# First layer norm and first projection of a two-layer transformer, written as one part

## The reference

```python
def _layernorm(x, axis=-1, eps=1e-05):
    m = jnp.mean(x, axis=axis, keepdims=True)
    v = jnp.var(x, axis=axis, keepdims=True)
    return (x - m) / jnp.sqrt(v + eps)
...
Q = (x @ W_q).reshape(b, s, N_HEADS, HEAD_DIM).transpose(0, 2, 1, 3)
K = (x @ W_k).reshape(b, s, N_KV_HEADS, HEAD_DIM).transpose(0, 2, 1, 3)
V = (x @ W_v).reshape(b, s, N_KV_HEADS, HEAD_DIM).transpose(0, 2, 1, 3)
Qr = _apply_rope(Q, positions)
...
Kr = _apply_rope(K_rep, positions)
```

## Time and profile before

| what | us |
|---|---|
| median of 3 runs | 2762.9 |
| lowest and highest run | 2759.66, 2764.67 |
| span of the profiled execution, first to last instruction | 2757.8 |
| median less span: what lies around the span | 5.1 |
| tensor engine busy | 2526.8 (92%) |
| vector engine busy | 1757.1 (64%) |
| from the start to the tensor engine's first instruction | 20.48 |
| from the start to the first product of the projection | 43.38 |
| from the start to the first tensor work of `heads0` | 141.15 |

### The profile page before, as it was taken

How to read it: one execution, slowest core, us unless ns; L and a number is a source line. 1 busy time by engine, 2 the same in 40 slices (tenths; PEclk the granted TensorE clock), 3 DMA queues, 4 the chain that set the end, 5 groups by cost and what they waited for, 6 DMA issues and landing times. The chain is left out here.

```text
span 2757.8 us, 35900 instructions
## 1 busy us (share of the span) xinstructions
PE 2526.8 (92%) x12212; PEld 1711.0 (62%) x12212; DVE 1757.1 (64%) x4109; ACT 1080.5 (39%) x2566; POOL 1022.2 (37%) x756
## 2 busy tenths in 40 slices
PE   5889989898869999999697999978999979999998
PEld 2334434343348888888575777756777656667886
DVE  4647757575435555555545999956999923335886
ACT  2125535353522333222223777725777721111111
POOL 2217758584911111110003676624445410001442
PEclk9969999999979999999899999999999999999999
DMA  7371211111020000000211101010000078883201
GB/s 252 131 180 24 54 24 40 26 35 31 2 106 16 16 15 15 15 16 1 85 50 54 62 29 28 23 40 24 9 9 16 1 259 295 295 294 93 58 24 62
DMA packets 167335, 193.64 MB, mean 70 GB/s; under 512 B 51982, under 2 KB 114446, under 8 KB 166784
## 3 DMA queue, kind: packets, MB, share of 16 engines
q1 hardware_dynamic: 155648, 178.90, 20.8%
q0 software_dynamic: 11520, 12.64, 1.4%
HBM read 161.95 MB, written 54.53 MB: 78 GB/s over the span
## 5 line engine op out<-in xcount | busy, mean ns | idle before, releaser
L621 DVE TENSOR_REDUCE mx<-bank 128x1 f32<-128x512 f32 x512 | 327.9, 679 | 121.7 <-PE bank L528 115.5
L468 POOL TENSOR_TENSOR probs<-probs 128x1024 f32<-128x1024 f32 x128 | 301.5, 2376 | 211.2 <-PE bank L551 174.0
L679 ACT ACTIVATE probs<-bank 128x1024 f32<-128x1024 f32 x256 | 250.1, 1022 | 271.8 <-PE bank L541 271.8
L1475 POOL TENSOR_SCALAR mix<-mix,sm 128x256 f32<-128x256 f32 (+1 forms) x256 | 232.5, 919 | 175.1 <-DVE sm L1372 174.9
L1415 ACT ACTIVATE ms<-ms,sm 128x256 f32<-128x256 f32 (+1 forms) x512 | 247.6, 486 | 93.9 <-DVE sm L1343 92.9
L528 PE MATMUL bank<-k_parts,q_parts 96*128 96x512 f32 x512 | 219.8, 476 | 7.3 <-DVE X L644 3.3
L528 PEld LDWEIGHTS bank<-k_parts,q_parts 96*128 96x128 f32 x512 | 94.0, 196 | 171.4 <-DVE mx L621 139.1
L855 POOL TENSOR_TENSOR up_lo<-up_raw,up_hi 128x1024 fp32r<-128x1024 f32 x16 | 46.2, 2907 | 401.0 <-ACT up_hi L845 401.0
L1343 DVE CUSTOM_DVE_ANT_0 ms<-bank,misc 128x256 f32<-128x256 f32 (+1 forms) x512 | 184.7, 399 | 2.3
L541 PE MATMUL bank<-q_parts,k_parts 97*128 97x512 f32 x512 | 148.4, 406 | 15.8 <-ACT probs L679 8.9
L925 DVE TENSOR_TENSOR hid<-bank,sg 128x512 f32<-128x512 f32 x64 | 44.2, 691 | 180.2 <-ACT sg L875 180.2
(11 more groups left out here) (221 smaller groups left out, 5863.4 us busy)
## 6 DMA issues: line engine op xcount, KB each, us to landing
ewg<-in_L_ffn_Wg_dram SPq DMA_DIRECT2D x32, 704.0 KB, 6.8
ewu<-in_L_ffn_Wu_dram SPq DMA_DIRECT2D x32, 704.0 KB, 8.0
ewd<-in_L_ffn_Wd_dram SPq DMA_DIRECT2D x32, 512.0 KB, 5.2
q_parts<-qk_dram SPq DMA_DIRECT2D x48, 256.0 KB, 4.4
up_raw<-in_L_ffn_W_dram SPq DMA_DIRECT2D x16, 512.0 KB, 4.1
ewd<-in_L_ffn_Wd_dram SPq DMA_DIRECT2D x32, 192.0 KB, 5.3
qk_dram<-qk_hi SPq DMA_DIRECT2D x4, 1280.0 KB, 5.1
qk_dram<-qk_lo SPq DMA_DIRECT2D x4, 1280.0 KB, 7.2
```

The source lines that it names most:

```text
L468: pool.tensor_tensor(probs[:, even, half, :], probs[:, even, half, :], probs[:, odd, half, :], ALU.add).then_inc(S["paired"], 1)
L621: dve.reduce_max(mx[:, U % 2, q, h:h + 1], bank[:, h, :], AX.X).then_inc(S["max"], 1)
L679: act.activation(probs[:, s % BUFS, 2 * x:2 * x + 2, :], bank[:, 2 + 2 * x:4 + 2 * x, :], ACT.Exp, scale=scale).then_inc(S["exps"], 1)
L1475: pool.tensor_scalar(mix[:, p % 2, h, 0:w], mix[:, p % 2, h, 0:w], sm[:, p % 3, 8 + h:9 + h], None, ALU.mult).then_inc(S["probs"], 1)
```

## The change: two blocks become one

The call of `layer_norm` ahead of `attention0` is gone; its work stands in `project0`. The second layer's `layer_norm` keeps its instructions, with the branches for the first one taken out. In the new block:

- The sync engine issues all loads at its start: X quarter 0, misc, the three weights, rope, X quarters 1 to 3, then the output weight and the second feed-forward weight.
- Moments, square root and reciprocal are taken per quarter of four tiles. For quarter 0 they run first, then its four tiles are normalised and transposed, and the products begin when the weights are there; rope is waited for apart, by the vector engine (`cos_in`).
- For quarter c+1 the vector engine takes the moments after turn 0 of quarter c, the reciprocal and two tiles after turn 1, one tile after turn 2 and one after turn 3. The tensor engine transposes one tile after each of the products 2 to 5, into two banks of their own (4 and 5).
- The values of quarter c are transposed after product 1 of quarter c+1, no longer at the end of quarter c.
- GpSimd issues the 16 clearing DMAs in quarter 2, three or four after each low half.

```diff
-            layer_norm(env, "0", first=True)
             attention0(env)
...
+            rows(0)
+            sp.dma_start(env["misc"][:, :], env["consts"]["misc"]).then_inc(consts_loaded, 16)
             for c0, c1, name in ((0, D, "W_q"), (D, D + P, "W_k"), (D + P, D + 2 * P, "W_v")):
                 sp.dma_start(w[:, :, c0:c1], ins["L0_attn_" + name].rearrange("(k p) n -> p k n", p=P)).then_inc(S["w"], 16)
-            sp.dma_start(rope[:, :, :], env["consts"]["rope0"].rearrange("p (a s) -> p a s", a=2)).then_inc(S["w"], 16)
+            sp.dma_start(rope[:, :, :], env["consts"]["rope0"].rearrange("p (a s) -> p a s", a=2)).then_inc(S["cos_in"], 16)
+            for c in range(1, NC):
+                rows(c)
...
         @block.tensor
         def _(pe):
-            wait(pe, S["w"], 64)
...
+            def turn_rows(n):
+                pe.wait_ge(xn_ready, n + 1)
+                if n >= 2:
+                    pe.wait_ge(xt_taken, n - 1)
+                for k in range(KD):
+                    mm = pe.transpose(bank[:, 4 + n % 2, k * P:(k + 1) * P], xn[:, n % 2, k * P:(k + 1) * P], ident)
+                mm.then_inc(xt_ready, 1)
...
+            pe.wait_ge(consts_loaded, 16)
+            for n in range(SUBS):
+                turn_rows(n)
+            wait(pe, S["w"], 48)
+            for c in range(NC):
+                pe.wait_ge(xt_taken, SUBS * (c + 1))
+                for f in range(NF):
+                    product(c, f)
+                    if f == 1 and c:
+                        turn_values(c - 1)
+                    if f >= 2 and c + 1 < NC:
+                        turn_rows(SUBS * (c + 1) + f - 2)
+            turn_values(NC - 1)
...
+            moments(0)
+            inverse(0)
+            for n in range(SUBS):
+                normal(n)
+            wait(dve, S["cos_in"], 16)
             for c in range(NC):
...
+                more = c + 1 < NC
+                for f in range(NR):
+                    turn(c, f)
+                    if more and f == 0:
+                        moments(c + 1)
+                    if more and f == 1:
+                        inverse(c + 1)
+                        normal(SUBS * (c + 1))
+                        normal(SUBS * (c + 1) + 1)
+                    if more and f in (2, 3):
+                        normal(SUBS * (c + 1) + f)
+                wait(dve, S["proj"], c * NF + NF)
+                wait(dve, S["v_rows"], c)
+                dve.tensor_copy(vT[:, :], bank[:, NR % 4, :]).then_inc(S["read"], 1)
...
                     wait(pool, S["hi"], c * NR + f + 1)
                     pool.tensor_tensor(lo[:, c % 2, f, :], rot[:, f % 2, :], hi[:, c % 2, f, :].bitcast(F32),
                                        ALU.subtract).then_inc(S["lo"], 1)
+                    if c == 2:
+                        for m in range(3 * f, min(3 * f + 4 if f == NR - 1 else 3 * f + 3, SLOTS // P)):
+                            pool.dma_start(env["xe"][m * P:(m + 1) * P, :], zero[:, :]).then_inc(zeroed, 16)
```

More of the change, by code:

```diff
@@ L144, in build, with layer_norm @@
             feed_forward1(env, r)
[L147 to L154, removed]
+def layer_norm(env, xn, r):
+    nc, X, bank, ident, sem = (env[k] for k in ("nc", "X", "bank", "ident", "sem"))
@@ L155, in layer_norm @@
     stats_done, aggr_done, var_done, sd_done, rstd_done, xn_ready, xt_ready, xt_taken = env["ln"]
-    once, tiles = (0, 0) if first else (1, NT)
-    high_done = sem("ln_high" + tag) if rows is not None else None
-    QL = len(x_loaded)
+    once, tiles = NC, NT
+    high_done = sem("ln_high")
     with ExitStack() as ctx:
[L160 to L166, removed]
-        block = ctx.enter_context(nc.Block())
[L169 to L209, removed]
@@ L323, in _ @@
         def _(pe):
-            wait(pe, S["w"], 64)
-            for c in range(NC):
-                for f in range(NF):
-                    wait(pe, S["read"], c * NF + f - (1 if f < NF - 4 else 3))
-                    for k in range(KD):
-                        mm = pe.matmul(bank[:, f % 4, :], w[:, k, f * P:(f + 1) * P],
-                                       xnT[:, k, c * CH:(c + 1) * CH], start=(k == 0), stop=(k == KD - 1))
-                    mm.then_inc(S["proj"], 1)
+            def turn_rows(n):
+                pe.wait_ge(xn_ready, n + 1)
+                if n >= 2:
+                    pe.wait_ge(xt_taken, n - 1)
+                for k in range(KD):
+                    mm = pe.transpose(bank[:, 4 + n % 2, k * P:(k + 1) * P], xn[:, n % 2, k * P:(k + 1) * P], ident)
+                mm.then_inc(xt_ready, 1)
@@ L333, in _, with product, turn_values @@
+            def product(c, f):
+                wait(pe, S["read"], c * NF + f - (1 if f < NF - 4 else 3))
+                for k in range(KD):
+                    mm = pe.matmul(bank[:, f % 4, :], w[:, k, f * P:(f + 1) * P],
+                                   xnT[:, k, c * CH:(c + 1) * CH], start=(k == 0), stop=(k == KD - 1))
+                mm.then_inc(S["proj"], 1)
+            def turn_values(c):
                 wait(pe, S["read"], c * NF + NF)
                 wait(pe, S["v_taken"], c)
-                for s in range(CH // P):
+                for s in range(SUBS):
@@ new lines, in turn @@
+            def turn(c, f):
+                at = slice(c % 2 * CH, c % 2 * CH + CH)
+                n = c * NR + f
+                wait(dve, S["proj"], c * NF + f + 1)
+                wait(dve, S["rotated"], n)
+                dve.tensor_tensor(direct[:, f % 2, :], bank[:, f % 4, :], rope[:, 0, at],
+                                  ALU.mult).then_inc(S["cos"], 1)
+                dve.stream_shuffle(swapped[:, f % 2, :], bank[:, f % 4, :],
+                                   [i ^ 1 for i in range(32)]).then_inc(S["read"], 1)
+                wait(dve, S["read"], c * NF + f + 1)
+                dve.tensor_tensor(swapped[:, f % 2, :], swapped[:, f % 2, :], rope[:, 1, at],
+                                  ALU.mult).then_inc(S["sin"], 1)
+                wait(dve, S["sin"], n + 1)
+                wait(dve, S["lo"], n - 1 if f else n)
+                dve.tensor_tensor(rot[:, f % 2, :], direct[:, f % 2, :], swapped[:, f % 2, :],
+                                  ALU.add).then_inc(S["rotated"], 1)
@@ L366, in _, with take_values @@
+            def take_values(c):
+                wait(act, S["v_rows"], c + 1)
+                act.activation(t["v"][:, c * SUBS:(c + 1) * SUBS, :, :],
+                               bank[:, 6, :].rearrange("p (s j d) -> p s j d", j=KV0, d=HD0),
+                               ACT.Copy).then_inc(S["v_taken"], 1)
+            root(0)
+            for n in range(SUBS):
+                take_rows(n)
             for c in range(NC):
+                more = c + 1 < NC
                 if c > 1:
```

140 lines of the change are left out of this document (91 added, 49 removed).

## The result

The changed kernel takes 2746.89 us (median of 4 runs, 2745.86 to 2747.07), the kernel before 2762.78 in the same comparison (4 runs): a ratio of 0.9946, 95% interval 0.9935 to 0.9958. That is faster, by 15.9 us. The forecast was 2746. The profiled execution of the changed kernel took 2746.78, with a span (first to last instruction) of 2745.0.

What follows compares the result with a forecast made beforehand. The tensor engine bounds the kernel on average (92% busy) but has little to do for some 30 us at the start; -28.8 - 1.2 + 12.15 + 0.5 = -17.35 from the 2757.8 span, plus 5.1, gave 2746 us, range 2738 to 2757.

Steps and rivals of the forecast that it cites:

- Part 1, up to the first product: Start of the kernel: first row transpose at 10.2, first product at 14.6 instead of 43.38, a term of -28.8 us.
- Part 2, the clock: First product: most of its time at half clock goes, a term of -1.2 us, between 0 and -1.65.
- Part 3, a quarter: Projection: each quarter that prepares the next takes 26.1 us instead of 22.05, +12.15 for three, bounds +2.9 to +15.
- Part 4, the end: Last quarter of the projection: prepares nothing but has quarter 2's values' transposes in its middle, +0.5 us.
- The clock falls in the stall: Rival: tensor engine's 2.2 us wait behind product 2 drops the clock, at least 1.65 us three times: 2751, up to 2756; 14%.
- a fall of the granted clock inside the projection: Sign in the projection that would make the prediction wrong; it expected a granted clock of 1.00 soon after the first product.
- No stall: Rival in the projection's quarters: the moments hide wholly in the vector engine's idle time, 3 x 2.2 us less: 2739; 5%.
- Not in order of issue: Rival at the start: weights land with the last loads, first product at 36, 21 of 28.8 us lost: 2767; 4%.
- GpSimd's issues are held up: Rival in quarter 2: clearing DMA issues slow beside turns, deciding from 1.5 us each; at 3.5 us, 24 us: 2770; 4%.
- The Trainium skill's rule: Rule against the change: some vector instructions hold a port GpSimd needs for DMA descriptors, so its issues in quarter 2 could stall.
- the last line of the sum: Whole kernel: -17.35 from the profiled span of 2757.8 gives 2740.4; adding 5.1 from span to median gives 2746.

Runs made afterwards that it cites:

- X first: Changed kernel with all four quarters of X loaded first, then misc, the weights and the rope table: 2752.57 us, ratio 0.9968 to the kernel before.
- the repeat: The changed kernel run again with no edit: 2745.4 us, ratio 0.9939 to the kernel before.
- the kernel with the rows earlier: Changed kernel with moments before turn 0 in all quarters, reciprocal and two tiles after it, row transposes one product earlier except in quarter 0: 2737.51 us.
- the moments a turn earlier: Changed kernel with the next quarter's moments and square root before turn 0 in quarters 1 and 2, quarter 0 unchanged: 2741.6 us, ratio 0.9929.
- the first execution of before: First profiled execution of the unaltered kernel before: 2759.66 us, 2616.6 of it from heads0 to the end of the span.
- before's own third: Third profiled execution of the unaltered kernel before: 2762.18 us, 2618.0 of it from heads0 to the end of the span.
- the second of before: Second profiled execution of the unaltered kernel before: 2759.56 us, 2616.3 of it from heads0 to the end of the span.
- the last experiment: The kernel before profiled twice more with no edit, for the 4 us behind heads0: 2759.56 and 2762.18 us.

## Why the prediction was right, and where it was not

**Part 1, up to the first product: right.** First row transpose 10.37 for 10.2, first product 14.71 for 14.6: -28.7 for -28.8. The loads landed in the order of issue, the last weight at 12.0 for 11.4; the experiment with X first shows what the order is worth.

**Part 2, the clock: right in kind, in one execution of two.** The half clock that 5.29 us of the first product showed is gone in the profiled execution, 1.5 us for the 1.2 forecast. In the repeat 1.8 us were lost to a late rise, so the term was about nil there, the other end of its bounds.

**Part 3, a quarter: right in its parts.** 25.79 for 26.1. The row transposes took 0.43 each (25.05 to 25.48 in the timeline of the kernel with the rows earlier) for 0.49, the stall added 2.0 for 2.2 (1.82 of it idle), the end 0.86 for 0.87 (0.69 of it idle). Moving the moments alone, which the prediction blamed, takes the stall away. Quarter 0 was forecast to stall 0.5 longer than the others, and it did (2.31 against 1.82); it took 27.34 because the clock fell there.

**Part 4, the end: right.** From the last product 0 to `heads0` 30.58 us, before 30.04: 0.54 for 0.5. The sum of the four parts at `heads0` was -17.35; it is -16.95 in the first execution.

**Rivals.** "The clock falls in the stall" came true once in three stalls and cost 1.5 us, near its price of 1.65. It was not the outcome, since the shorter stalls of 1.82 left the clock up in all executions. But the prediction had named a fall of the granted clock inside the projection as a sign that it was wrong, and that sign came, in quarter 0: the forecast held because one fall costs 1.5 us, and not because there was none. "No stall" is refuted by the rows, and the moments a turn earlier show what it would have taken. "Not in order of issue" falls with X first. "GpSimd's issues are held up": their mean is 0.563 us (0.539 to 0.753, 16 issues) for the 0.571 of the earlier trace rows, where 1.5 us each were needed to decide, and the vector engine never waits for a low half. The Trainium skill's rule (SBUF — State Buffer, section "SBUF: two separate sides"), by which such issues stall behind some vector instructions, does not show on them here. On the low halves something like it may: the one at 80.68, which starts while the vector engine normalises two tiles (80.06 to 81.06), took 1.52 us for 1.27, as the two others behind a turn 1 did.

**The step that was off** is the last line of the sum: "so 2740.4; the median lies 5.1 above the span, so 2746". It took everything behind `heads0` to move rigidly, at the 2616.6 us of the first execution of before; there it was 2620.8, and 2618.0 in before's own third. And it took the 5.1 for something around the span. An execution is only 1.8 us longer than its own span (2746.78 and 2745.0 for the changed kernel, 2759.56 and 2757.8 for the second of before); by that the first profiled execution of before, with its span of 2757.8, was the fastest of its runs, 2759.66. The other 3.3 were the distance of before's median from its fastest run, and the changed kernel's median lies 0.1 above its profiled run. So the sum lacked 4.2 us behind `heads0`, 0.4 ahead of it and the 0.1, and had 3.3 too many; that leaves 1.4, of which the forecast's rounding from 2745.5 to 2746 took 0.5. Of the 4.2, the last experiment finds 1.5 and 1.0 at two places that before's third execution has too; the rest is not put down to places. The start was forecast to half a microsecond; that the total came out as near is partly luck, since two errors of opposite sign met.

## What to carry to other kernels

When loads stand in one queue, issue them as early as the program can, in the order in which their first users want them. Issuing the weights and the rope table a block earlier alone brought 11.4 of the 17 us at `heads0`. Putting 3 MB that were not needed yet ahead of the rest cost 5.6 back, and it was a small table with the identity matrix that came too late. When two conditions of a wait are met within 0.1 us, the name that the profile gives says little. When work is moved into the idle time of an engine that is not the bound, write out one period instruction by instruction and look for the first thing the bounding engine wants from it: here nine small instructions a turn too late cost some 2 us in each of three periods, though the vector engine had room. A forecast made against one profiled execution has to say how far that execution lies from its own median, and to add only the launch, not that distance, to the span of another kernel.

## What the hardware did that was not expected

The same wait of the tensor engine let the clock fall in one execution and not in another: 2.31 or 2.32 us behind product 2 of quarter 0, a fall in three of four executions (the changed kernel, the moments earlier, X first; not in the repeat), at 1.5 to 1.7 us each; 3.40 us ahead of the products of the second attention's keys and values, a fall in six of nine, at 1.5 us each in these products. None of the six waits of 1.82 in the same stage let it fall. So a wait of this size can cost over a microsecond more than it lasts, and two kernels that differ by one or two microseconds have to be compared over several executions.
